# A four-layer graph network on one core: layer 3's passes over the edges get another order of work on each engine, a loop body of ten turns, and five shared PSUM banks in between

## The chip, the core and the metric

One core of a Trainium2 chip runs the whole program, 108212 recorded instructions. The metric is the device time of one execution in microseconds (us). TensorE is called PE here, VectorE DVE, ScalarE ACT, GpSimd POOL, and SyncE, which issues transfers, SP. An engine name with a q (DVEq) is that engine's sequencer, which handles register instructions, loads into registers and branches.

## What is computed

Four layers over a graph of N = 3125 nodes with 256 features and E = 50000 edges sorted by target. The change touches the graph part of layer 3, two rounds of this:

```python
k = (x @ Wk).reshape(n, H, D)   # H = 32 heads, D = 8
q = (x @ Wq).reshape(n, H, D)
v = (x @ Wv).reshape(n, H, D)
k_e, q_e, v_e = k[src], q[dst], v[src]
kw = where(is0, einsum('ehd,hdf->ehf', k_e, Watt[:, 0]), einsum(..., Watt[:, 1]))
m  = where(is0, einsum('ehd,hdf->ehf', v_e, Wmsg[:, 0]), einsum(..., Wmsg[:, 1]))
a  = (kw * q_e).sum(-1) * pri[:, etype].T / sqrt(D)
ea = exp(a - segment_max(a, dst)[dst])
att = ea / segment_sum(ea, dst)[dst]
h = segment_sum(m * att[:, :, None], dst).reshape(n, H * D) @ Wa
x = h * alpha + x * (1 - alpha)
```

## The kernel before

`hgt` runs each of the two rounds as an edge pass (`edge_pass` with kind "hgt"), a short join, and `renew`, which for the first round also makes the next round's table of keys and values and its queries. Gathered rows already hold the keys and messages of both edge types multiplied out, so a pass only gathers, scores, weighs and sums.

**The pass.** The 50000 edges lie in 416 tiles of 128, four tiles to a chunk, 104 chunks; one chunk is one turn. The work of turn k goes through the engines so: POOL gathers the chunk's rows from HBM into a ring `g` of NB = 4 chunks. SP fetches `locrow`, 256 KB (`hot`, line 764), and the masks. ACT turns `hot` into one-hot columns (lines 846 and 848). PE picks the queries with them (`queries`, line 805, eight matmuls, into `found`). DVE multiplies keys and queries (line 923) and sums by head (line 925). PE turns the scores into rows (line 813). DVE takes running maxima forwards and backwards (`scan` line 932, `scan_back` line 936). PE turns them back (line 820). DVE subtracts (`less`, lines 966 and 967), ACT takes exponents (line 861), DVE weighs the messages (`weigh`, line 974). PE sums them by node (`total`, line 831, eight matmuls in two halves), ACT copies the sums out of PSUM into `stage` (`take`, line 872), SP stores two of them (`keep`, line 769), and DVE adds them to the block of nodes in `acc` that the tile belongs to (`add`, line 988, four a turn). The block's number is loaded into a register from memory (`blocks_of`, line 667, one TENSOR_LOAD for all four), and each addition waits on a semaphore for the addition before it.

**The order.** Each engine has its order written out by hand, in `piped`: a list of stages, each with a lag in turns. Here is a turn of DVE before, as written:

```python
piped(v, NCH, [now(score), add(0), now(scan), add(1), now(scan_back), add(2), now(less), add(3), now(weigh(0))], NB)
```

`piped` writes the first turns out, then a hardware loop (`Fori`) whose body holds `unroll` turns, then the last ones. `unroll` was NB, so 4 turns here; layer 2's pass has a body of 8 turns, layer 0's one of 4. Translated, a body of DVE's has 133 instructions here, 494 in layer 2's pass and 239 or 247 in layer 0's two. `v.drain()` makes DVE wait until its own earlier operations have written their results.

**The renewal between the passes.** `renew` runs over 25 tiles of 125 nodes, in steps. PE transposes the sums (line 1961), multiplies by Wa (1969), transposes the new x (1977) and makes the 1280 new columns in three cuts of 512, 512 and 256 (1990, six matmuls a tile). DVE and ACT copy the cuts out of PSUM, and DVE counts s_take when its copies are done; PE waits for it and for ACT's s_half before the next tile's products, since there is one set of three banks. DVE also adds the old x (line 2105), between PE's 1969 and 1977.

Of the kernel before, what the change touches and what calls it, by code (L numbers as in the profile page):

```python
# [14 lines left out]
P = 125  # L15
# [31 lines left out]
def piped(eng, count, stages, unroll=4):  # L47
# [11 lines left out]
    with eng.Fori(first // unroll, last // unroll) as k:  # L59
        for u in range(unroll):  # L60
            step(unroll * k + u, u)
# [611 lines left out]
def edge_pass(core, name, kind, H, CT, acc, refs, crow, table, idx, look=None, early=None):  # L673
# [4 lines left out]
    NB = 8 if kind == "ee" else 4  # L678
# [7 lines left out]
    with Phase(core, name) as ph:  # L686
# [92 lines left out]
        def _(pe):  # L779
# [18 lines left out]
            def queries(k, b):  # L798
                blks = list(asked)
                pe.wait_ge(s_hot, k + 1)  # L800
                if later(k, 1):
                    pe.wait_ge(s_prod, k)
                for h in range(2):
                    for j in range(HT):
                        mm = pe.matmul(found[:, h, j * D:j * D + D], hot[0:P, b % 2, 128 * (h * HT + j):128 * (h * HT + j) + 128],  # L805
                                       look[:, bass.ds(blks[h * HT + j], 1), :].rearrange("p o c -> p (o c)"), start=True, stop=True)
                mm.then_inc(s_found, 1)
# [14 lines left out]
            def total(h):  # L822
                def body(k, b):
# [4 lines left out]
                    for t in range(h * HT, h * HT + HT):  # L828
                        if later(k, 1) or t >= 4:
                            pe.wait_ge(s_staged if kind == "hgt" else s_added, CT * k + t - 3)  # L830
                        pe.matmul(out[:, t % 4, 0:WO], here[:, b % 2, t, :], g[:, b, t, F:F + WO], start=True, stop=True).then_inc(s_out, 1)  # L831
# [3 lines left out]
            if kind == "ee":  # L835
                piped(pe, NCH, [(0, turn), (0, turn_back), (1, total(0)), (1, total(1))], NB)
            elif kind == "gat":
                piped(pe, NCH, [(1, turn), (2, total(0)), (1, turn_back), (0, find), (2, total(1))], NB)
            else:
                piped(pe, NCH, [(2, total(0)), (0, whose), (1, turn), (2, total(1)), (1, turn_back), (0, queries)], NB)  # L840

        @block.scalar
        def _(act):
# [32 lines left out]
            if kind == "gat":  # L876
                piped(act, NCH, [(3, take(0)), (2, exponent), (3, take(1)), (0, one_hot)], NB)
            elif kind == "hgt":
                piped(act, NCH, [(3, take(0)), (3, take(1)), (2, exponent), (0, one_hot), (1, rows_here)], NB)
            else:  # L880
                piped(act, NCH, [(0, exponent), (1, take(0)), (1, take(1))], NB)

        @block.vector
        def _(v):
# [16 lines left out]

            def score(k, b):
                v.wait_ge(s_g[b], every(k, b, NB, 16 * CT))
# [4 lines left out]
                if kind == "gat":  # L908
# [3 lines left out]
                    v.tensor_tensor(sums[:, :, :], sums[:, :, :], g[:, b, :, D:D + H], ALU.add)  # L912
# [2496 lines left out]
```

## Time and profile before

| | |
|---|---|
| median of 3 runs | 7328.54 us (7322.5 to 7334.62) |
| the profiled execution | 7332.78 us |
| its span on the core | 7330.6 us |
| granted TensorE clock, mean of the span | 0.867 of full |
| busy share: PE, DVE, ACT, POOL | 69%, 64%, 40%, 48% |

The first pass of layer 3 lies about between 4890 and 5626 us of the span, the renewal between 5703 and 5907, the second pass between 5907 and 6641. In a row of a timeline the columns are start, duration, engine, line, operation, out<-in, and in brackets the idle time before it with what ended it; durations of neighbours overlap a little, so that the distance between two starts is what an operation takes of the engine.

### The profile page before, as it was taken

The page shows a single profiled execution, that of the slowest core. Times are in us where ns is not written, and L with a number is a line of the kernel's source. Part 1 is how long each engine was busy: PE and PEld are TensorE (multiplying, and loading weights), DVE is VectorE, ACT ScalarE, POOL GpSimd, SP SyncE. Part 2 cuts the span into 40 slices and gives each one's busy share as a digit, 9 for nine tenths or more (in the row PEclk, how much of TensorE's full clock was granted, in tenths as well). Part 3 has the DMA queues.
Part 4 walks back from the last instruction along what each step waited for, and adds up shares of the span by engine and source line. Part 5 has one row for each costly group of instructions (what it writes and reads, how often), then busy time and mean ns, then how long its engine had stood idle before and what let it go on. Part 6 is the DMA issues. An engine that isn't in the chain of part 4 may idle for free. (4 is left out here: it accounts for less than half of the span.)

```text
span 7330.6 us, 108212 instructions
## 1 busy us (share of the span) xinstructions
PE 5055.0 (69%) x21503; PEld 3608.8 (49%) x21504; DVE 4711.4 (64%) x11833; ACT 2945.6 (40%) x7221; POOL 3519.8 (48%) x3532
## 2 busy tenths in 40 slices
PE   4763777767765967769666667777776767776764
PEld 4763444444444834558544457644444444444453
DVE  6876577667775168550566662379997379995453
ACT  2552355455544220022223332237775157773331
POOL 1776377447730267731167703336663056660014
PEclk9999977777777988979877778999999999997887
DMA  3442344334423943339334417756664167761036
GB/s 89 165 140 69 97 128 128 69 104 127 127 58 112 310 110 101 103 75 334 115 96 107 106 39 257 243 166 212 211 210 122 50 181 212 211 210 45 18 120 197
DMA packets 523817, 1021.67 MB, mean 139 GB/s; under 512 B 143645, under 2 KB 284498, under 8 KB 514846
## 3 DMA queue, kind: packets, MB, share of 16 engines
q0 software_dynamic: 191360, 489.21, 24.6%
q1 hardware_dynamic: 301663, 497.07, 21.0%
q10 hardware_dynamic: 30528, 32.52, 1.3%
q8 instruction: 86, 1.41, 0.1%
q14 instruction: 180, 1.47, 0.1%
HBM read 927.97 MB, written 90.27 MB: 139 GB/s over the span
## 5 line engine op out<-in xcount | busy, mean ns | idle before, releaser
L733 POOL DMA_INDIRECT l_hgt_ep_g<-l_tkm,l_hgt_ep_ix x832 | 922.4, 1109 | 441.3 <-PE l_hgt_ep_out L831 237.6
L744 POOL DMA_INDIRECT l_gat_ep_g<-l_gat_th,keep_e_src x832 | 863.4, 1038 | 439.8 <-issue 232.2
L831 PE MATMUL l_gat_ep_out<-l_gat_ep_g,l_gat_ep_here 128*126 128x264 f32 x1664 | 712.0, 570 | 137.4 <-DVE l_gat_acc L988 131.9
L831 PEld LDWEIGHTS l_gat_ep_out<-l_gat_ep_g,l_gat_ep_here 128*126 128x126 f32 x1664 | 387.8, 264 | 369.0 <-DVE l_gat_acc L988 301.7
L2495 DVE TENSOR_TENSOR f_moe_experts_yb<-f_moe_experts_py,f_moe_experts_b2s 128x256 f32<-128x256 f32 x208 | 88.4, 425 | 719.7 <-PE f_moe_experts_py L2478 700.7
L831 PE MATMUL l_hgt_ep_out<-l_hgt_ep_g,l_hgt_ep_here 128*126 128x288 f32 x1664 | 500.4, 424 | 53.8 <-DVE l_hgt_ep_g L974 52.3
L2446 POOL DMA_INDIRECT f_moe_experts_xg<-f_moe_tx,f_moe_tok x208 | 197.3, 949 | 708.2 <-PE f_moe_experts_px L2459 625.2
L872 ACT COPY l_gat_ep_stage<-l_gat_ep_out 30x264 f32<-30x264 f32 x832 | 306.3, 371 | 524.5 <-PE l_gat_ep_out L831 516.7
L2510 ACT ACTIVATE f_moe_experts_ht<-f_moe_experts_phid,f_moe_experts_b1b 128x128 f32<-128x128 f32 x848 | 241.3, 372 | 673.1 <-PE f_moe_experts_phid L2469 671.5
L525 POOL DMA_INDIRECT recs<-place_stage,place_pos x392 | 424.8, 1084 | 138.5 <-issue 117.1
L2831 POOL DMA_INDIRECT l_edges_g<-l_table,keep_e_src x416 | 412.3, 991 | 146.8 <-issue 119.8
L2469 PE MATMUL f_moe_experts_phid<-f_moe_experts_xt,f_moe_experts_w1b 128*128 128x128 f32 x3392 | 429.9, 281 | 74.5 <-DMA f_moe_experts_b1b<-in_L_ffn_b 66.3
L744 POOL DMA_INDIRECT l_ep_g<-l_table,keep_e_src x416 | 408.3, 982 | 126.6 <-issue 117.8
L2469 PEld LDWEIGHTS f_moe_experts_phid<-f_moe_experts_xt,f_moe_experts_w1b 128*128 128x128 f32 x3392 | 403.6, 195 | 95.8 <-issue 63.7
L805 PE MATMUL l_hgt_ep_found<-l_q,l_hgt_ep_hot 125*128 x1664 | 425.5, 400 | 26.0 <-ACT l_hgt_ep_hot L848 21.0
L2478 PE MATMUL f_moe_experts_py<-f_moe_experts_w2b,f_moe_experts_ht 128*128 128x256 f32 x1696 | 402.7, 381 | 0.0
L872 ACT COPY l_hgt_ep_stage<-l_hgt_ep_out 126x288 f32<-126x288 f32 x832 | 307.2, 394 | 218.3 <-PE l_hgt_ep_out L831 207.3
L988 DVE TENSOR_TENSOR l_gat_acc<-l_gat_acc,l_gat_ep_out 125x264 f32 x832 | 344.2, 414 | 68.8 <-issue 48.7
L988 DVE TENSOR_TENSOR l_hgt_acc<-l_hgt_acc,l_hgt_ep_stage 125x288 f32 x832 | 370.1, 445 | 20.9 <-ACT l_hgt_ep_stage L872 13.8
L831 PEld LDWEIGHTS l_hgt_ep_out<-l_hgt_ep_g,l_hgt_ep_here 128*126 128x126 f32 x1664 | 284.6, 190 | 181.1 <-issue 133.1
L2843 PE MATMUL l_edges_out<-l_edges_g,l_edges_here 128*125 128x256 f32 x832 | 254.1, 452 | 151.2 <-DVE l_acc L2930 49.0
L805 PEld LDWEIGHTS l_hgt_ep_found<-l_q,l_hgt_ep_hot 125*128 125x128 f32 x1664 | 306.5, 194 | 99.4 <-issue 62.9
(652 smaller groups left out, 11794.6 us busy)
## 6 DMA issues: line engine op xcount, KB each, us to landing
l_hgt_ep_hot<-locrow SPq DMA_DIRECT2D x208, 256.0 KB, 4.8
f_moe_experts_w1b<-in_L_ffn_w SPq DMA_DIRECT2D x32, 1024.0 KB
f_moe_experts_w2b<-in_L_ffn_w SPq DMA_DIRECT2D x32, 1024.0 KB
f_moe_experts_w1b<-in_L_ffn_w SPq DMA_DIRECT2D x64, 512.0 KB, 5.0
f_moe_experts_w2b<-in_L_ffn_w SPq DMA_DIRECT2D x64, 512.0 KB, 5.2
f_moe_experts_w1b<-in_L_ffn_W SPq DMA_DIRECT2D x56, 512.0 KB
f_moe_experts_w2b<-in_L_ffn_W SPq DMA_DIRECT2D x56, 512.0 KB
l_gat_ep_hot<-locrow SPq DMA_DIRECT2D x104, 256.0 KB
```

The costliest lines, as they stand in the source:

```text
L525: gp.indirect_dma_start(recs, bass.IndirectOffsetOnAxis(ap=pos[:, b, j:j + 1].bitcast(U32), axis=0), stage[:, b, j, :], None).then_inc(sca ...
L733: gp.indirect_dma_start(g[:, b % NB, j, 0:W], None, table, bass.IndirectOffsetOnAxis(ap=ix[:, b, j:j + 1].bitcast(U32), axis=0)).then_inc( ...
L744: gp.indirect_dma_start(g[:, k % NB, j, 0:W], None, table, bass.IndirectOffsetOnAxis(ap=idx[:, k * CT + j:k * CT + j + 1].bitcast(U32), ax ...
L805: mm = pe.matmul(found[:, h, j * D:j * D + D], hot[0:P, b % 2, 128 * (h * HT + j):128 * (h * HT + j) + 128], look[:, bass.ds(blks[h * HT + ...
L831: pe.matmul(out[:, t % 4, 0:WO], here[:, b % 2, t, :], g[:, b, t, F:F + WO], start=True, stop=True).then_inc(s_out, 1)
L872: act.copy(stage[lo:P + 1, b % 2, t, :], out[lo:P + 1, t % 4, 0:WO]).then_inc(s_staged, 1)
L988: v.tensor_tensor(slot, slot, stage[0:P, b % 2, t, :] if kind == "hgt" else out[0:P, t % 4, 0:WO], ALU.add).then_inc(s_added, 1)
L2469: mm = pe.matmul(phid[:, b % 2, 128 * f:128 * f + 128], w1b[:, b, k, 128 * f:128 * f + 128], xt[:, b % 2, k, :], start=(k == 0), stop=(k = ...
L2478: mm = pe.matmul(py[:, b % 2, 0:D], ht[:, b % 2, f, :], w2b[:, b, f, :], start=(f == 0), stop=(f == FC - 1))
L2510: act.activation(ht[:, b % 2, f, :], phid[:, b % 2, 128 * f:128 * f + 128], func, bias=b1b[:, b, f:f + 1])
L2831: gp.indirect_dma_start(g[:, i % RB, j, :], None, table, bass.IndirectOffsetOnAxis(ap=core.e_src[:, i * EG + j:i * EG + j + 1].bitcast(U32 ...
L2843: pe.matmul(out[:, j, 0:D], here[:, i % 4, j, :], g[:, i % RB, j, :], start=True, stop=True).then_inc(s_out, 1)
```

## The change

A turn of DVE: the chunk's messages are weighed one turn later, right behind the next chunk's scores; the additions stand in pairs behind `scan_back` and behind `less`, tiles 2 and 3 one turn later than before, and each pair loads its own two block numbers. PE makes the queries in two halves, one before the rows are turned and one at the turn's end, and its sums in halves one turn later. ACT copies one half of the sums first in its turn and the other one before the exponents. The ring `g` has five chunks, and the loop's body ten turns, with 350 instructions on DVE. POOL's and SP's orders and lags stay. In the renewal the five banks of PSUM that hold cuts are given out in turn, (3t + n) mod 5, each cut with a semaphore of its own, and the two other products have one bank each where they had one or two.

```diff
-    NB = 8 if kind == "ee" else 4
+    NB = {"ee": 8, "gat": 4, "hgt": 5}[kind]
+    UN = 10 if kind == "hgt" else NB
...
-            def queries(k, b):
-                blks = list(asked)
-                pe.wait_ge(s_hot, k + 1)
-                if later(k, 1):
-                    pe.wait_ge(s_prod, k)
-                for h in range(2):
+            def queries(h):
+                def body(k, b):
+                    if h == 0:
+                        pe.wait_ge(s_hot, k + 1)
+                        if later(k, 1):
+                            pe.wait_ge(s_prod, k)
...
-                mm.then_inc(s_found, 1)
+                    if h == 1:
+                        mm.then_inc(s_found, 1)
+                return body
...
-                piped(pe, NCH, [(2, total(0)), (0, whose), (1, turn), (2, total(1)), (1, turn_back), (0, queries)], NB)
+                piped(pe, NCH, [(3, total(1)), (0, whose), (0, queries(0)), (1, turn), (2, total(0)), (1, turn_back), (0, queries(1))], UN)
...
-                piped(act, NCH, [(3, take(0)), (3, take(1)), (2, exponent), (0, one_hot), (1, rows_here)], NB)
+                piped(act, NCH, [(4, take(1)), (2, rows_here), (3, take(0)), (2, exponent), (0, one_hot)], UN)
...
-                    v.drain()
-                    v.tensor_reduce(r, g[:, b, :, 0:D].rearrange("p t (h d) -> p t h d", h=H), AX.X, ALU.add).then_inc(s_raw, 1)
+
+            def by_head(k, b):
+                v.drain()
+                v.tensor_reduce(raw[:, b % 2, :, :], g[:, b % NB, :, 0:D].rearrange("p t (h d) -> p t h d", h=H), AX.X, ALU.add).then_inc(s_raw, 1)
...
-                    n = HT if kind != "hgt" else CT
-                    if t % n == 0:
-                        blks[t:t + n] = blocks_of(core, mybir.EngineType.DVE, k * CT + t, n)
+                    if t % HT == 0:
+                        blks[t:t + HT] = blocks_of(core, mybir.EngineType.DVE, k * CT + t, HT)
...
-                return (2 if t >= HT and kind != "hgt" else 1), body
+                return (2 if t >= HT else 1), body
...
-                piped(v, NCH, [now(score), add(0), now(scan), add(1), now(scan_back), add(2), now(less), add(3), now(weigh(0))], NB)
+                piped(v, NCH, [now(score), now(by_head), (1, weigh(0)), now(scan), now(scan_back), add(2), add(3), now(less), add(0), add(1)], UN, turns)
...
-                        if t >= B1:
+                        if t >= B1 and not shared:
                             pe.wait_ge(s_take, t - B1 + 1)
...
+                            if shared and len(cuts) * t + n >= 5:
+                                before, cut = divmod(len(cuts) * t + n - 5, len(cuts))
+                                pe.wait_ge((s_first, s_half, s_take)[cut], before + 1)
```

On DVE, in the loop of the passes, a turn stood so before (ISA here is a register instruction, TENSOR_LOAD the load of block numbers):

```order
L923 TENSOR_TENSOR l_hgt_ep_g<-l_hgt_ep_g,l_hgt_ep_found 128x4x256
L925 TENSOR_REDUCE l_hgt_ep_raw<-l_hgt_ep_g 128x128
L667 ISA
L667 TENSOR_LOAD keep_e_blk
L984 REGISTER_ALU
L988 ISA
L988 TENSOR_TENSOR l_hgt_acc<-l_hgt_acc,l_hgt_ep_stage 125x288
L932 SCALAR_TENSOR_TENSOR l_hgt_ep_fwd<-l_hgt_ep_masks,l_hgt_ep_rows 128x128
L984 REGISTER_ALU
L988 ISA
L988 TENSOR_TENSOR l_hgt_acc<-l_hgt_acc,l_hgt_ep_stage 125x288
L936 SCALAR_TENSOR_TENSOR l_hgt_ep_top<-l_hgt_ep_masks,l_hgt_ep_fwd 128x128
```

and after `scan_back` came:

```order
L984 REGISTER_ALU
L988 ISA
L988 TENSOR_TENSOR l_hgt_acc<-l_hgt_acc,l_hgt_ep_stage 125x288
L966 TENSOR_TENSOR l_hgt_ep_x<-l_hgt_ep_raw,l_hgt_ep_back 128x128
L967 ISA
L967 COPY l_hgt_refs<-l_hgt_ep_top 128x2
L984 REGISTER_ALU
L988 ISA
L988 TENSOR_TENSOR l_hgt_acc<-l_hgt_acc,l_hgt_ep_stage 125x288
L974 TENSOR_TENSOR l_hgt_ep_g<-l_hgt_ep_g 128x4x256
```

After the change a turn begins so (lines are 10 to 13 higher):

```order
L933 TENSOR_TENSOR l_hgt_ep_g<-l_hgt_ep_g,l_hgt_ep_found 128x4x256
L937 TENSOR_REDUCE l_hgt_ep_raw<-l_hgt_ep_g 128x128
L986 TENSOR_TENSOR l_hgt_ep_g<-l_hgt_ep_g 128x4x256
L941 ISA
L944 SCALAR_TENSOR_TENSOR l_hgt_ep_fwd<-l_hgt_ep_masks,l_hgt_ep_rows 128x128
L948 SCALAR_TENSOR_TENSOR l_hgt_ep_top<-l_hgt_ep_masks,l_hgt_ep_fwd 128x128
L669 ISA
L669 TENSOR_LOAD keep_e_blk
L995 REGISTER_ALU
L999 ISA
L999 TENSOR_TENSOR l_hgt_acc<-l_hgt_acc,l_hgt_ep_stage 125x288
L995 REGISTER_ALU
```

and ends so:

```order
L999 TENSOR_TENSOR l_hgt_acc<-l_hgt_acc,l_hgt_ep_stage 125x288
L978 TENSOR_TENSOR l_hgt_ep_x<-l_hgt_ep_raw,l_hgt_ep_back 128x128
L979 ISA
L979 COPY l_hgt_refs<-l_hgt_ep_top 128x2
L669 ISA
L669 TENSOR_LOAD keep_e_blk
L995 REGISTER_ALU
L999 ISA
L999 TENSOR_TENSOR l_hgt_acc<-l_hgt_acc,l_hgt_ep_stage 125x288
L995 REGISTER_ALU
L999 ISA
L999 TENSOR_TENSOR l_hgt_acc<-l_hgt_acc,l_hgt_ep_stage 125x288
```

The weighing has moved up behind the reduction, and the additions, each of which stood between two other operations, stand in two pairs. The one load behind the reduction has become two, one behind `scan_back` and one behind the copy.

On PE a turn of the loop stood so before:

```order
L831 MATMUL l_hgt_ep_out<-l_hgt_ep_g,l_hgt_ep_here 126x288
L667 ISA
L667 TENSOR_LOAD keep_e_blk
L813 MATMUL l_hgt_ep_rows<-keep_ident,l_hgt_ep_raw 128x128
L830 REGISTER_ALU
L831 MATMUL l_hgt_ep_out<-l_hgt_ep_g,l_hgt_ep_here 126x288 x2
L820 MATMUL l_hgt_ep_back<-keep_ident,l_hgt_ep_top 128x128
L800 REGISTER_ALU
L805 ISA
L805 MATMUL l_hgt_ep_found<-l_q,l_hgt_ep_hot 128x256
L805 ISA
L805 MATMUL l_hgt_ep_found<-l_q,l_hgt_ep_hot 128x256
```

and stands so now:

```order
L804 REGISTER_ALU
L808 ISA
L808 MATMUL l_hgt_ep_found<-l_q,l_hgt_ep_hot 128x256
L808 ISA
L808 MATMUL l_hgt_ep_found<-l_q,l_hgt_ep_hot 128x256
L817 REGISTER_ALU
L818 MATMUL l_hgt_ep_rows<-keep_ident,l_hgt_ep_raw 128x128
L835 ISA
L836 MATMUL l_hgt_ep_out<-l_hgt_ep_g,l_hgt_ep_here 126x288
L835 REGISTER_ALU
L836 MATMUL l_hgt_ep_out<-l_hgt_ep_g,l_hgt_ep_here 126x288
L825 MATMUL l_hgt_ep_back<-keep_ident,l_hgt_ep_top 128x128
```

Two of the four products of the queries (L808) have moved ahead of the turned rows (L818); the other two come right behind the last row shown, behind the turned maxima (L825), where all four stood before (L805, the first two shown).

## Rows read from the trace of the kernel before

**Rows 1.** Windows of the trace: the first pass, and the renewal between passes (busy us, clock).

```profile
4890.00:5626.00 736.00, 512.04 (x1873) 318.75 (x1874) 663.17 (x1145) 513.94 (x1249) 486.69 (x518) 0.98 0.68 205
5703.00:5907.00 204.00, 153.36 (x500) 87.96 (x500) 54.33 (x103) 30.76 (x75) 0.00 (x0) 0.94 0.20 62
```

**Rows 2.** Groups by line on DVE, 4950 to 5550: busy, mean ns, idle before.

```profile
L988 DVE TENSOR_TENSOR l_hgt_acc<-l_hgt_acc,l_hgt_ep_stage 125x288 f32 x351 | 155.8, 444 | 3.6 <-ACT l_hgt_ep_stage L872 0.8
L925 DVE TENSOR_REDUCE l_hgt_ep_raw<-l_hgt_ep_g 128x128 f32<-128x1024 f32 x88 | 107.4, 1220 | 8.0
...
L932 DVE TENSOR_TENSOR_SCAN l_hgt_ep_fwd<-l_hgt_ep_masks,l_hgt_ep_rows 128x128 f32<-128x128 f32 x88 | 37.0, 421 | 7.6 <-PE l_hgt_ep_rows L813 3.9
```

**Rows 3.** Timeline of DVE, one turn: start, duration, operation.

```profile
5208.49 1.22 DVE L923 TENSOR_TENSOR l_hgt_ep_g<-l_hgt_ep_g,l_hgt_ep_found 128x1024 f32<-128x1024 f32 x1
5209.81 1.22 DVE L925 TENSOR_REDUCE l_hgt_ep_raw<-l_hgt_ep_g 128x128 f32<-128x1024 f32 x1
5210.94 0.45 DVE L988 TENSOR_TENSOR l_hgt_acc<-l_hgt_acc,l_hgt_ep_stage 125x288 f32 x1
5211.45 0.42 DVE L932 TENSOR_TENSOR_SCAN l_hgt_ep_fwd<-l_hgt_ep_masks,l_hgt_ep_rows 128x128 f32<-128x128 f32 x1
...
5212.31 0.42 DVE L936 TENSOR_TENSOR_SCAN l_hgt_ep_top<-l_hgt_ep_masks,l_hgt_ep_fwd 128x128 f32<-128x128 f32 x1
5212.65 0.43 DVE L988 TENSOR_TENSOR l_hgt_acc<-l_hgt_acc,l_hgt_ep_stage 125x288 f32 x1
5213.22 0.29 DVE L966 TENSOR_TENSOR l_hgt_ep_x<-l_hgt_ep_raw,l_hgt_ep_back 128x128 f32<-128x128 f32 x1
...
5213.61 0.46 DVE L988 TENSOR_TENSOR l_hgt_acc<-l_hgt_acc,l_hgt_ep_stage 125x288 f32 x1
5213.99 1.22 DVE L974 TENSOR_TENSOR l_hgt_ep_g<-l_hgt_ep_g 128x1024 f32<-128x1024 f32 x1
5215.23 1.22 DVE L923 TENSOR_TENSOR l_hgt_ep_g<-l_hgt_ep_g,l_hgt_ep_found 128x1024 f32<-128x1024 f32 x1
```

**Rows 4.** Timeline of DVE in layer 0's pass: a load behind a short operation.

```profile
1613.84 0.19 DVE L914 SCALAR_TENSOR_TENSOR l_gat_ep_raw<-l_gat_ep_sums 128x32 f32<-128x32 f32 x1
1614.43 0.43 DVE L988 TENSOR_TENSOR l_gat_acc<-l_gat_acc,l_gat_ep_out 125x264 f32 x1 [0.40 <-issue]
```

**Rows 5.** Instructions of line 667, 4950 to 5550: ns least, median, most.

```profile
L667 DVEq TENSOR_LOAD <-keep_e_blk x88: 339/344/357, 4950.0 to 5546.7; - x88
```

**Rows 6.** Timeline of DVE in layer 0's pass: additions in a row.

```profile
1398.87 0.43 DVE L988 TENSOR_TENSOR l_gat_acc<-l_gat_acc,l_gat_ep_out 125x264 f32 x1 [0.21 <-DVE l_gat_acc L988]
1399.51 0.43 DVE L988 TENSOR_TENSOR l_gat_acc<-l_gat_acc,l_gat_ep_out 125x264 f32 x1 [0.21 <-DVE l_gat_acc L988]
```

**Rows 7.** Instructions of line 59 (loop), layer 2's pass: ns, start us.

```profile
L59 DVEq COMPARE_BRANCH  x1: 73/73/73, 3947.8 to 3947.8; - x1
...
L59 DVEq FUSED_REGOPS  x1: 80/80/80, 3950.8 to 3950.8; - x1
```

**Rows 8.** The same line in layer 3's first pass.

```profile
L59 DVEq COMPARE_BRANCH  x1: 56/56/56, 5008.8 to 5008.8; - x1
L59 DVEq FUSED_REGOPS  x1: 74/74/74, 5009.2 to 5009.2; - x1
```

**Rows 9.** Line 764's transfer of locrow, 5000 to 5580: us to landing.

```profile
DMA to landing us min/median/max: 3.5/4.8/6.4
```

**Rows 10.** Groups by line on ACT, 4950 to 5550.

```profile
L872 ACT COPY l_hgt_ep_stage<-l_hgt_ep_out 126x288 f32<-126x288 f32 x352 | 129.9, 394 | 89.1 <-PE l_hgt_ep_out L831 84.8
...
L848 ACT ACTIVATE l_hgt_ep_hot<-l_hgt_ep_hot,keep_ones 128x512 f32<-128x512 f32 x87 | 62.8, 722 | 6.0
```

**Rows 11.** Timeline of PE in the renewal: two starts of one tile's products.

```profile
5780.39 4.53 PE L1990 MATMUL l_hgt_out_out<-l_w,l_hgt_out_xt 128*125 128x512 f32 x12 [1.62 <-DVEq L2154]
...
5787.84 0.67 PE L1990 MATMUL l_hgt_out_out<-l_w,l_hgt_out_xt 128*125 128x512 f32 x1 [1.62 <-DVEq L2154]
```

**Rows 12.** The same, late in the renewal.

```profile
5888.54 4.53 PE L1990 MATMUL l_hgt_out_out<-l_w,l_hgt_out_xt 128*125 128x512 f32 x12 [1.04 <-ACT l_hgt_out_rows L2026]
```

More of the change, by code:

```diff
@@ L44, in later, with piped @@
     return not isinstance(i, int) or i >= n
-def piped(eng, count, stages, unroll=4):
+def piped(eng, count, stages, unroll=4, turns=None):
     first = -(-(max(lag for lag, _ in stages) + unroll) // unroll) * unroll
@@ L59, in piped @@
     with eng.Fori(first // unroll, last // unroll) as k:
+        if turns is not None:
+            turns[:] = [k]
         for u in range(unroll):
@@ L830, in body @@
                             pe.wait_ge(s_staged if kind == "hgt" else s_added, CT * k + t - 3)
-                        pe.matmul(out[:, t % 4, 0:WO], here[:, b % 2, t, :], g[:, b, t, F:F + WO], start=True, stop=True).then_inc(s_out, 1)
+                        pe.matmul(out[:, t % 4, 0:WO], here[:, b % 2, t, :], g[:, b % NB, t, F:F + WO], start=True, stop=True).then_inc(s_out, 1)
                 return body
@@ L900, in _ @@
             v.drain()
+            turns = [None]
             def score(k, b):
-                v.wait_ge(s_g[b], every(k, b, NB, 16 * CT))
+                if isinstance(k, int):
+                    v.wait_ge(s_g[b % NB], 16 * CT * (k // NB + 1))
+                else:
+                    v.wait_ge(s_g[b % NB], turns[0] * (16 * CT * UN // NB) + 16 * CT * (b // NB + 1))
                 if later(k):
@@ L1854, in renew @@
     mixed = part["acc"] if part else xn
-    B0, B1 = (1, 1) if part and wide else (2, 2)
+    shared = part is not None and wide
+    B0, B1 = 1 if shared else 2, 2
     last_on_vector = onward.get("last") if wide else None
@@ L1892, in renew, with made_in @@
             xt1 = kept_xt if kept_xt is not None else ph.sb("xt1", [128, 2, 2, P])
-            pt1 = ph.psum("pt1", [128, 2, 512])
-            out1 = ph.psum("out1", [P, B1, len(cuts), 512])
+            pt1 = ph.psum("pt1", [128, B0, 512])
+            out1 = ph.psum("out1", [P, 1, 5, 512] if shared else [P, B1, len(cuts), 512])
+            s_cut = [ph.sem(f"cut{n}") for n in range(2)] if shared else []
+            s_first = ph.sem("first") if shared else None
+            def made_in(t, n, c):
+                return out1[:, 0, (len(cuts) * t + n) % 5, 0:c] if shared else out1[:, t % B1, n, 0:c]
             w, dst = onward["w"], onward["dst"]
@@ L2104, in _ @@
                         v.wait_ge(s_mm0, t + 1)
-                        o = v.scalar_tensor_tensor(out=x[:, t, :], in0=part["old"][:, t, :], scalar=part["rest"], in1=out0[:, t % 2, 0:D], op0=ALU.mult, op1=ALU.add)
+                        o = v.scalar_tensor_tensor(out=x[:, t, :], in0=part["old"][:, t, :], scalar=part["rest"], in1=out0[:, t % B0, 0:D], op0=ALU.mult, op1=ALU.add)
                         if back is not None:
```

66 lines of the change are left out of this document (36 added, 30 removed).

## The prediction

> **What bounds the kernel now.** The page gives no engine more than 69% of the span, so I looked only at the stretches that the change touches. The view by windows shows a pass of 736.00 us in which DVE is busy 663.17 and PE 512.04, at clock 0.98, and a renewal of 204.00 in which PE is busy 153.36 and DVE only 54.33 [rows 1]. The groups by line then show that DVE in the pass waits almost for nothing: the 351 additions have 3.6 us of idle time before them in 600 us, the reduction comes 88 times with 8.0, and the scan waits 3.9 of its 7.6 us for PE [rows 2]. So a turn is 600/88 = 6.82 us, and it is the sum of DVE's own row of instructions. The timeline of one turn reads it off [rows 3]: from the product at 5208.49 to the next one at 5215.23, 6.74 us. What DVE's order costs is what the passes cost, 2 x 104 turns.
>
> **A turn, laid out anew.** I take distances between starts from [rows 3].
> - Product to reduction, with the drain between them, stays 1.32.
> - The weighing behind the reduction: reduction to the next start was 1.13, take 1.14. It starts at 2.45.
> - The scan behind the weighing: the weighing is as large as the reduction, another 1.14, start 3.59. Its rows have been turned meanwhile: PE had 0.51 us for that before (addition 5210.94 to scan 5211.45) and has 1.14 now. That ends the wait for PE.
> - scan_back behind the scan and a drain: the scan takes 0.42, and the drain a little more, start 4.09.
> - First addition of the pair (tile 2). Before it stands a load of two block numbers that nothing covers. A load takes 339 to 357 ns on DVE's sequencer [rows 5]. Before, it lay under the reduction of 1.22 us. Now it comes behind scan_back, whose 0.42 us are too short for load, register arithmetic and the wait on a semaphore. Layer 0's pass has the same place: an operation of 0.19 us at 1613.84, a load, and the addition only at 1614.43, with 0.40 idle [rows 4], so that the chain from one start to the other is 0.59. Here the register arithmetic of `acc`'s address and the wait for `stage` may come on top: at most as much again as a load, 0.34, so between 0.59 and 0.93. I take the middle, an estimate of 0.755, against 0.34 before (5212.31 to 5212.65). Start 4.845; **+0.41** for the load.
> - Second addition (tile 3). It waits for the semaphore of the one before it. In layer 0's pass, where additions stand in a row, each has 0.21 idle before it and starts 0.64 behind the last [rows 6], where the distance between an addition and another operation is 0.34 to 0.38 here [rows 3]. The old order had another operation of 0.29 or more between any two additions. Start 5.485; **+0.29**.
> - less 0.35 later, 5.835 (before, from 5212.65 to 5213.22, it came 0.57 behind the addition: 0.22 was a wait for PE's turned-back maxima, which is gone: **-0.22**). Less and copy together take 0.39 (to the addition at 5213.61).
> - First addition of the second pair (tile 0): another load, issued when the copy has been handed over, about 5.65; by the chain of 0.755 with two operations in a row handed over it starts at about 6.5, against 6.25 (5.835 + 0.39) without a load: **+0.25**.
> - Second addition (tile 1): 0.64 behind, 7.15; **+0.29**.
> - Next product 0.36 behind: 7.50. Gone are what the scan waited (0.13 to 0.2) and the 0.1 by which the weighing and the next product stood further apart than 1.14 (5213.99 to 5215.23).
>
> Old turn 6.82, plus 0.41 + 0.29 + 0.25 + 0.29 = 1.24, minus 0.22, 0.16, 0.10 and some 0.1 that the drained scan_back gains without an addition ahead of it, is about 7.5. I take 7.50; the bounds: both loads hidden 6.95 to 7.0, and both chains as long as with nothing below them 7.7.
>
> **Another ring stands close.** ACT's take of the second half is now first in its turn, behind the one-hot. SP keeps its order, so that the store of tile 3 of chunk k-3 stands ahead of the next fetch of locrow. That makes one ring a turn: take 0.7 (two of 0.394), fetch 4.8 to landing (3.5 to 6.4), one-hot two of 0.722, with issue 1.5 [rows 9, 10], and about 0.65 of stores' issue: 7.65 with 4.8, 6.35 with 3.5, 9.25 with 6.4. Before, the same ring took two turns of DVE. So 7.50 may become a little more; I take 7.55 as a mean, +0.72 for each of the 80 loop turns of a pass, 2 x 80 x 0.72 = **+115**. The other 24 turns of a pass are written out; they load and wait alike, but I leave out what the fetch ring adds and a part of the second load: 2 x 24 x 0.55 = **+26**.
>
> **The loop's end.** The body of ten turns has 350 instructions on DVE, and the jump back is taken 7 times a pass. In layer 2's pass, with 494, the branch at 3947.8 is followed by the next register instruction only at 3950.8, 2.9 us of nothing [rows 7]; in layer 3's with 133, from 5008.8 to 5009.2 [rows 8]. 350 lies between the two, and no row tells on which side. [...] Its 2.9 us and some 0.4 until the turn is back in step, 3.3, come 14 times: **+46**; at the short one's price it is +7. The old loop ended 24 times a pass with some 0.2 us, which the new one does 7 times: **-6**.
> [...]
>
> **The renewal.** PE begins one tile's products at 5780.39 and the next at 5787.84, 7.45 apart, with 1.62 idle right before, ended by DVE's count of its copies [rows 11]; late in the stretch the wait is 1.04 [rows 12]. With five banks the first cut of the next tile needs only a bank that was emptied a tile before. Both waits go; what PE has of its own is 7.45 - 1.62 = 5.83. Of 25 tiles the first five run while the line fills: 15 x 1.62 + 4 x 1.04 = 28, and where one wait is gone the copies at the end run sooner and PE's gap behind DVE's addition of the old x closes a little: I take **-37**, between -30 and -42. What hides there is nothing: PE is the bound of that stretch.
>
> Ring of five chunks: POOL is busy 486.69 of 736.00 [rows 1] and no DVE row waits for a gather, so it gives nothing. Queries in halves: no DVE row of a turn waits for them.
>
> **Sum.** 115 + 26 + 46 - 6 - 37 = +144 on the profiled execution's 7332.78, 7477; the median of the runs shown lies 4 lower, so 7473. I say **7470**.
>
> **Rivals.**
> - *Faster.* The waits that go (for rows, for turned-back maxima, before the product) are worth 0.5, and the loads lie under their neighbours because the sequencer runs ahead. If also half of the self-waits is hidden, a turn takes 6.5: 208 x -0.32 = -67, and -37 gives 7225; with a turn as before only the renewal is left, 7292. It decides where the turn stays below 6.82 + 37/208 = 7.00 (without misses). Against it stand both costs, shown in the same operation [rows 4, 6]. 0.13.
> - *No change.* Loads hidden, self-waits only: a turn of 6.85, +6, +46 for the jumps, -37: 7343; 0.05.
> - *The fetch ring or PE sets the turn.* With landings near 6 us a turn is 8 to 8.3: 160 x 1.3 + 26 + 46 - 43 = +237, 7566. For it: 256 KB a turn beside the gathers. Against it: the median of 4.8, and fewer transfers per us in a slower turn. 0.12.
> - *The jump is cheap*, all else as forecast: -39, 7431. [...] Within the forecast's range: 0.25.
> - The forecast itself, with misses: 0.45.
>
> **How the numbers follow.** About 0.2% (15 us) is what a measurement can tell from no change. Slower: 0.45 + 0.25 + 0.12 = 0.82; same 0.05; faster 0.13. The bounds of the turn, 7.3 to 7.7, and of the jumps give 7390 to 7510 for the likeliest; to reach 8 in 10 the range takes in some of the ring's case: 7365 to 7560.
>
> **What the new profile would show.** The first addition behind scan_back 0.7 to 0.8 us after scan_back's start, with about 0.3 idle; the second with 0.21 idle ended by DVE's own addition; no scan row that waits for PE; a gap of 3 us on DVE every ten turns; DVE busy less than before in a longer pass; steps of 5.8 us in the renewal. I would be wrong if additions in pairs stand 0.35 apart, if the load's 0.34 us don't show, or if the one-hot waits for its transfer in most turns.

## The result, and the profile after

The changed kernel takes 7608.79 us (median of 4, 7607.7 to 7613.77) where the kernel before takes 7330.1 on the same chip: 1.0381 of it, with a 95% interval of 1.0365 to 1.0398. The forecast was 7470, in a range of 7365 to 7560; the kernel became slower, as forecast, but by 279 us in place of 140, and lies outside the range. One later execution of the changed kernel (in e5) took 8743.67 us at a granted clock of 0.575; the comparisons rest on the others.

The profiled execution has a span of 7606.5 us against 7330.6, 275.9 more. Measured from DVE's first key product (line 923 before, 933 after) to its last one, a pass has grown from 713.9 to 875.9 us and from 708.6 to 867.9, together by 321. The stretch between the passes has shrunk from 306.7 to 264.4. The rest of the program, before and after, makes -3. So everything lies where the change is, and the two parts of it have opposite signs.

The windows of the first pass, the counterpart of [rows 1] (busy us with counts, granted clock, share of the DMA engines, GB/s):

```profile
4901.00:5777.00 876.00, 588.04 (x1846) 386.31 (x1846) 656.28 (x1127) 508.95 (x1228) 478.39 (x510) 0.84 0.58 170
```

DVE is busy for about as long as before (656 against 663), but in 876 us in place of 736: it waits. PE does the same products in 588 where it had 512, at a granted clock of 0.84 in place of 0.98. Both were to be explained. What DVE waits for stands in its waits over the same stretch (us in total, times, longest):

```profile
DVE l_hgt_acc L999 <- issue: 102.6, 201, 1.1
DVE l_hgt_acc L999 <- DVE l_hgt_acc L999: 31.2, 145, 0.2
DVE l_hgt_ep_g L933 <- issue: 25.5, 7, 5.2
DVE l_hgt_ep_raw L937 <- issue: 14.4, 7, 2.9
DVE l_hgt_acc L999 <- ACT l_hgt_ep_stage L877: 13.1, 59, 0.7
DVE l_hgt_ep_x L978 <- PE l_hgt_ep_back L825: 12.1, 38, 1.1
```

Before, all these together had 3.6 us in front of the additions in 600 [rows 2]. Now the additions have 147 in 876, in three rows. The largest row says "issue", a wait for nothing that the profile shows, about twice a turn, half a microsecond each. The second is an addition that waits for the addition before it. The rows with 7 times are the seven jumps of the loop, and in this pass each jump has two of them. In the second pass (6030 to 6910) only the first of the two is there:

```profile
DVE l_hgt_ep_g L933 <- issue: 26.4, 7, 4.6
```

One turn on DVE, the counterpart of [rows 3] (start, duration, operation, idle before it):

```profile
5210.22 1.21 DVE L933 TENSOR_TENSOR l_hgt_ep_g<-l_hgt_ep_g,l_hgt_ep_found 128x1024 f32<-128x1024 f32 x1
5211.52 1.22 DVE L937 TENSOR_REDUCE l_hgt_ep_raw<-l_hgt_ep_g 128x128 f32<-128x1024 f32 x1
5212.66 1.22 DVE L986 TENSOR_TENSOR l_hgt_ep_g<-l_hgt_ep_g 128x1024 f32<-128x1024 f32 x1
5213.79 0.41 DVE L944 TENSOR_TENSOR_SCAN l_hgt_ep_fwd<-l_hgt_ep_masks,l_hgt_ep_rows 128x128 f32<-128x128 f32 x1
5214.28 0.42 DVE L948 TENSOR_TENSOR_SCAN l_hgt_ep_top<-l_hgt_ep_masks,l_hgt_ep_fwd 128x128 f32<-128x128 f32 x1
5215.21 0.46 DVE L999 TENSOR_TENSOR l_hgt_acc<-l_hgt_acc,l_hgt_ep_stage 125x288 f32 x1 [0.51 <-issue]
5215.89 0.46 DVE L999 TENSOR_TENSOR l_hgt_acc<-l_hgt_acc,l_hgt_ep_stage 125x288 f32 x1 [0.22 <-ACT l_hgt_ep_stage L877]
5216.27 0.28 DVE L978 TENSOR_TENSOR l_hgt_ep_x<-l_hgt_ep_raw,l_hgt_ep_back 128x128 f32<-128x128 f32 x1
5216.46 0.17 DVE L979 COPY l_hgt_refs<-l_hgt_ep_top 128x2 f32 x1
5217.07 0.46 DVE L999 TENSOR_TENSOR l_hgt_acc<-l_hgt_acc,l_hgt_ep_stage 125x288 f32 x1 [0.45 <-issue]
5217.75 0.46 DVE L999 TENSOR_TENSOR l_hgt_acc<-l_hgt_acc,l_hgt_ep_stage 125x288 f32 x1 [0.22 <-DVE l_hgt_acc L999]
5218.13 1.21 DVE L933 TENSOR_TENSOR l_hgt_ep_g<-l_hgt_ep_g,l_hgt_ep_found 128x1024 f32<-128x1024 f32 x1
```

It is 7.91 us. Up to scan_back at 4.06 behind the product it is the forecast's turn to a few hundredths. Then the first addition comes 0.93 behind scan_back (forecast 0.755), and the one behind the copy 0.61 behind it. The cause stands in the instructions of the line that loads the block numbers (ns least, median, most; DVEq is DVE's sequencer):

```profile
L669 DVEq TENSOR_LOAD <-keep_e_blk x127: 520/536/555, 5005.2 to 5549.3; - x127
...
L669 PEldq TENSOR_LOAD <-keep_e_blk x63: 328/332/352, 5006.0 to 5542.4; - x63
```

DVE's load of two numbers takes 0.536 us, where its load of four took 0.344 [rows 5]; PE's load, still of four, is where it was, at 0.332.

In other turns PE stands in the way. Here are PE's rows of the turn before, and of this one:

```profile
5205.56 2.28 PE L836 MATMUL l_hgt_ep_out<-l_hgt_ep_g,l_hgt_ep_here 128*126 128x288 f32 x4 [0.67 <-DVE l_hgt_ep_g L986]
5207.64 0.42 PE L825 MATMUL l_hgt_ep_back<-keep_ident,l_hgt_ep_top 128*128 128x128 f32 x1
...
5214.11 1.23 PE L836 MATMUL l_hgt_ep_out<-l_hgt_ep_g,l_hgt_ep_here 128*126 128x288 f32 x4 [0.98 <-DVE l_hgt_ep_g L986]
5215.18 0.27 PE L825 MATMUL l_hgt_ep_back<-keep_ident,l_hgt_ep_top 128*128 128x128 f32 x1
```

The same products (L836) take 2.28 and 1.23 us: the granted clock was 0.50 from 5205.5 to 5207.9 and 1.00 from 5214.0 to 5215.5. In the slow one the maxima are turned back so late that `less` waits 0.31 and the load behind it starts later; that turn is 8.55 us. I sorted the turns by the duration of the row L825 (0.42 and 0.27 in these two): 82 at the half clock have a mean of 8.38, 103 at the full one 7.905 (turns over 9.2 left out). Ahead of the half-clock rows PE had waited 2.3 us for DVE's product (median), ahead of the full-clock ones 1.2.

The end of a loop's body, on DVE's timeline:

```profile
5400.73 0.46 DVE L999 TENSOR_TENSOR l_hgt_acc<-l_hgt_acc,l_hgt_ep_stage 125x288 f32 x1 [0.22 <-DVE l_hgt_acc L999]
5404.90 1.22 DVE L933 TENSOR_TENSOR l_hgt_ep_g<-l_hgt_ep_g,l_hgt_ep_found 128x1024 f32<-128x1024 f32 x1 [3.71 <-issue]
5408.56 1.22 DVE L937 TENSOR_REDUCE l_hgt_ep_raw<-l_hgt_ep_g 128x128 f32<-128x1024 f32 x1 [2.43 <-issue]
```

Behind the branch at 5400.8 the next register instruction comes at 5404.5, and a few instructions on DVE stalls again: five instructions have run, and the sixth, the drain ahead of the reduction, starts only at 5408.4. The page's list of queues shows the same from another side: the queue of kind instruction, q14, has 267 packets where it had 180. Around this jump, from 5398 to 5412, it has three:

```profile
q14 instruction: 3, 0.02, 0.5%
```

In the trace they have 8192 bytes each and start at 5402.7, 5406.6 and 5409.1: one ahead of the first instruction behind the branch, one ahead of the drain. At all 14 jumps of the two passes the second packet behind the branch starts 2.4 to 4.5 us behind the first one, which has taken 0.3 to 0.7.

In the renewal, PE's rows of the five-bank rotation:

```profile
5931.90 4.46 PE L2010 MATMUL l_hgt_out_out<-l_w,l_hgt_out_xt 128*125 128x512 f32 x12
...
5937.50 4.46 PE L2010 MATMUL l_hgt_out_out<-l_w,l_hgt_out_xt 128*125 128x512 f32 x12
```

They begin 5.60 apart with no wait before them, where they began 7.45 apart [rows 11].

### The profile page after: what moved, and what is told of

Same layout as the page of the kernel before. It is cut to its first block and busy times, and to the rows that moved or that the text cites. A ratio compares the mean times of both kernels' runs of the same rounds, so it can differ in the third digit from the quotient of the medians.

```text
span 7606.5 us, 107407 instructions
## 1 busy us (share of the span) xinstructions
PE 5238.5 (69%) x21503; PEld 3766.9 (50%) x21504; DVE 4733.1 (62%) x11833; ACT 2955.5 (39%) x7221; POOL 3510.8 (46%) x3532
## 5 line engine op out<-in xcount | busy, mean ns | idle before, releaser
L736 POOL DMA_INDIRECT l_hgt_ep_g<-l_tkm,l_hgt_ep_ix x832 | 896.3, 1077 | 768.1 <-PE l_hgt_ep_out L836 538.0
L808 PE MATMUL l_hgt_ep_found<-l_q,l_hgt_ep_hot 125*128 x1664 | 551.4, 463 | 412.0 <-DVE l_hgt_ep_g L933 391.1
L836 PE MATMUL l_gat_ep_out<-l_gat_ep_g,l_gat_ep_here 128*126 128x264 f32 x1664 | 717.8, 576 | 136.2 <-DVE l_gat_acc L999 132.0
L836 PE MATMUL l_hgt_ep_out<-l_hgt_ep_g,l_hgt_ep_here 128*126 128x288 f32 x1664 | 619.9, 505 | 175.4 <-DVE l_hgt_ep_g L986 126.1
L808 PEld LDWEIGHTS l_hgt_ep_found<-l_q,l_hgt_ep_hot 125*128 125x128 f32 x1664 | 347.7, 232 | 582.8 <-issue 534.3
L836 PEld LDWEIGHTS l_gat_ep_out<-l_gat_ep_g,l_gat_ep_here 128*126 128x126 f32 x1664 | 389.2, 266 | 370.3 <-DVE l_gat_acc L999 306.2
L836 PEld LDWEIGHTS l_hgt_ep_out<-l_hgt_ep_g,l_hgt_ep_here 128*126 128x126 f32 x1664 | 368.3, 234 | 316.3 <-issue 197.2
```

What stands on the lines that cost most here:

```text
L736: gp.indirect_dma_start(g[:, b % NB, j, 0:W], None, table, bass.IndirectOffsetOnAxis(ap=ix[:, b, j:j + 1].bitcast(U32), axis=0)).then_inc( ...
L836: pe.matmul(out[:, t % 4, 0:WO], here[:, b % 2, t, :], g[:, b % NB, t, F:F + WO], start=True, stop=True).then_inc(s_out, 1)
```

## The experiments

Two chips ran the parts of the program that no kernel here touches slower than the others: that of e1 to e4 (the first pass began at 5437 us in place of 4899, the kernel before took 7919 us) and that of e12 (7931 us). In e4, whose passes have the old order, 24 of the 206 turns took over 8 us, where the kernel before had 4, and the passes took 1485 us in place of 1422.5. So of these runs the traces' turns are compared more than the totals. "Pass 1 + 2" below is measured from the first key product to the last, as above: 1422.5 before, 1743.9 after.

**e1, loads of four.** Each pair loads all four numbers of its chunk and uses two.

```diff
-                        blks[t:t + HT] = blocks_of(core, mybir.EngineType.DVE, k * CT + t, HT)
+                        blks[:] = blocks_of(core, mybir.EngineType.DVE, k * CT, CT)
```

> The changed kernel, but each pair of additions loads all four block numbers of its chunk and uses two. Theory A (a load of two numbers is itself the slow thing, 0.52 to 0.54 us where loads of four take 0.34): the loads fall to 0.34, the plain turn from 7.90 to about 7.52, the total by 208 x 0.38 = 79 us to about 7530. Rival B (what is exposed behind scan_back is the waiting for ACT's stage or register work, not the load's length): loads may change, the first addition of a pair stands where it stood, total 7609 within 15 us.

Measured: 8097.36, 1.0229 of before on its chip. The loads:

```profile
L669 DVEq TENSOR_LOAD <-keep_e_blk x120: 340/344/359, 5699.9 to 6199.1; - x120
```

They fall from 0.536 to 0.344 us though they fetch twice as much, and the plain turn from 7.90 to 7.42. Passes 1686, 58 less, with 24 turns over 9.2 us in them, up to 14.3. Theory A holds: it is the load of two that is slow. The address is no rival: one of the two loads of a turn reads from the same place in both kernels, and all 127 took 520 ns or more. Two loads shorter by 0.19 make 0.38 of the 0.48; the edit also saves a register instruction a turn (341 in a body in place of 350), and how much of the other 0.1 that is, no run separates. Why two numbers take longer than four, no run here shows.

**e2, ring and body of four.**

```diff
-    NB = {"ee": 8, "gat": 4, "hgt": 5}[kind]
-    UN = 10 if kind == "hgt" else NB
+    NB = {"ee": 8, "gat": 4, "hgt": 4}[kind]
+    UN = NB
```

> The changed kernel with a ring of four chunks and a loop body of four turns. Theory A (the jump back of the long body costs 5.5 us each, 7 a pass, in two stalls of fetching): the two idle stretches of DVE at a jump vanish, 14 x 5.5 = -77, and the short one's 0.2 comes 48 times, +10: about 7540. Rival B (the fifth chunk feeds the gathers in time, since weighing a turn later holds rows longer): DVE's products wait for gathers, the gain is lost or turned, 7600 or more.

Measured: 8110.01, 1.0239 of before. The stalls at the jumps are gone (no jump over 0.3 us), the turns stay 7.90 and 8.55. Passes 1706, 38 less (on that chip). The turn is as long with four chunks as with five, so the fifth chunk buys nothing.

**e3, sums twice.** The products of tiles 2 and 3 are made twice in each turn, the first ones for nothing.

```diff
+                        if kind == "hgt" and h == 1:
+                            pe.matmul(out[:, t % 4, 0:WO], here[:, b % 2, t, :], g[:, b % NB, t, F:F + WO], start=True, stop=True)
                         pe.matmul(out[:, t % 4, 0:WO], here[:, b % 2, t, :], g[:, b % NB, t, F:F + WO], start=True, stop=True).then_inc(s_out, 1)
```

> The changed kernel with PE's sums of tiles 2 and 3 of each chunk made twice (the same products into the same bank, the second one counted), so that PE has four products more in the stretch in which it waits for DVE's product. Theory A (every other turn is 8.55 instead of 7.90 because PE's granted clock falls to half in PE's idle stretches and its turned-back maxima come late): the granted clock in the pass rises from 0.83 to 0.95 or more, the turns of 8.55 mostly go, about 100 of them x 0.65: 7609 - 60 = 7550. Rival B (PE's amount of work is what is late): more turns of 8.55 and longer ones, 7640 or more.

Measured: 8177.59, 1.0309. The clock in the pass rises only to 0.87, and 58 turns of 170 are at the half clock, mean 8.36, against 112 at 7.92; but 36 turns are over 9.2 us (mean 11.4) in place of 21, and the passes take 1783. Neither theory's numbers came out. It was taken up again in e11 without the jumps.

**e4, the renewal alone.** The kernel before with the five banks: the changed kernel with

```diff
-    UN = 10 if kind == "hgt" else NB
+    UN = NB          # and a ring of 4
...
-  [now(score), now(by_head), (1, weigh(0)), now(scan), now(scan_back), add(2), add(3), now(less), add(0), add(1)]
+  [now(score), now(by_head), add(0), now(scan), add(1), now(scan_back), add(2), now(less), add(3), now(weigh(0))]
```

and the old orders of PE and ACT, one load of four and the old lag of the additions.

> The kernel before with only the renewal's five shared banks. The distance between the last product of pass 1 and the first of pass 2 was 306.7 before and is 264.5 after: if that is the banks alone, 7330 - 42 = 7288. Rival: part of the 42 is the pass's new end (fewer additions left over), then 7290 to 7310.

Measured: 7896.69, 0.9975 of before (0.9954 to 0.9996). Between the passes the trace has 263.9, against 264.4 in the changed kernel: the banks do all of it, 43 us. The total shows only 23, on a chip whose executions of one kernel spread by 48.

**e5, the changed kernel again**, as the measure for e6 to e8.

> The changed kernel itself once more, as the measure for the other three of this chip. Both theories: 0.5 to 4% slower than the kernel before; its turns in the trace as in the first profile, 7.90 at full clock and 8.4 at half, two stalls at each jump.

Measured: 7615.28, 1.0385 of the kernel before (7332.46). Turns as before: 83 at the half clock with 8.38, 101 at the full one with 7.92. As in the first profile, the seven jumps of the first pass have two stalls each and those of the second pass one each, not two everywhere as expected.

**e6, the old order with a long body.** The kernel before with the five banks and UN = 12, 396 instructions on DVE; against e4:

```diff
-    UN = NB
+    UN = 12 if kind == "hgt" else NB
```

> The kernel before with the five shared banks, and its old order of a turn, but a loop body of 12 turns (399 instructions on DVE), jump back 6 times a pass. Theory A (a long body must be fetched anew at each jump, 3.2 us at the branch and 2.3 us some instructions later): 12 x 5.5 = +66 against the renewal alone, less some 8 for the short jumps it no longer has: 0.8% over it, so about 7346 where that is 7288. Rival (the stalls belong to the new order, in which DVE has no work queued at a jump): no idle stretch over 1 us at the branch, same time as the renewal alone.

Measured: 7380.36, 1.0067 of before; without the long body it should have been 43 us under it. Passes 1509.8, 87 more than before, over ten jumps 8.7 us each, where 5.5 were expected. Most of its turns are 6.74 to 7.03 as before; at the jumps they are 10.7 to 11.3 in the first pass and 14.6 to 15.1 in the second, and 8.2 to 8.6 behind. In the second pass, and not in the first, a second stall of 3.2 to 3.4 us stands a few instructions behind the jump. The branch:

```profile
L59 DVEq COMPARE_BRANCH  x1: 68/68/68, 5149.0 to 5149.0; - x1
...
L59 DVEq FUSED_REGOPS  x1: 62/62/62, 5154.2 to 5154.2; - x1
```

So the stalls belong to the long body, in whatever order; the rival falls.

**e7, e1 and e2 together.**

> The changed kernel with both mended: loads of four numbers, ring and body of four. If load length, jumps and clock are all there is apart from the pairs' own waits: turn 7.43 at full clock, 8.3 at half clock in a quarter of the turns, mean 7.65, no stall at a jump; passes 2 x 103 x (8.47 - 7.65) = 169 us shorter than the changed kernel, still 100 us longer than before (pairs waiting on themselves, loads in the open). Rival (ring of four holds it back): mean turn 7.9 or more.

Measured: 7477.28, 1.0199 of before, some 135 under the changed kernel. Passes 1613.5, mean turn 7.83, 0.18 more than expected: 73 turns are still at the half clock, a third and not a quarter. The waits of its first pass:

```profile
DVE l_hgt_acc L1001 <- issue: 59.2, 199, 0.5
DVE l_hgt_acc L1001 <- DVE l_hgt_acc L1001: 40.2, 188, 0.2
```

Even loads of four stand in the open for 0.3 us each, and each pair waits for itself once, 0.21.

**e8, single additions.** Loads and additions as far as possible where something covers them, PE's queries ahead of its sums, all additions two turns behind with one load of four numbers, the store of tiles 2 and 3 one turn later, ring and body of four.

```diff
-  [now(score), now(by_head), (1, weigh(0)), now(scan), now(scan_back), add(2), add(3), now(less), add(0), add(1)]
+  [now(score), add(0), now(by_head), add(1), (1, weigh(0)), now(scan), now(scan_back), add(2), now(less), add(3)]
...
-  [(3, total(1)), (0, whose), (0, queries(0)), (1, turn), (2, total(0)), (1, turn_back), (0, queries(1))]
+  [(3, total(1)), (0, whose), (0, queries(0)), (1, turn), (0, queries(1)), (2, total(0)), (1, turn_back)]
```

> A version meant to be fast: weighing one turn later as in the change, but the four additions each between two other operations, one load of four numbers behind the product that covers it, all two turns behind; PE makes both halves of the queries ahead of the sums; the store of tiles 2 and 3 one turn later on SP; ring and body of four; five shared banks. If the loads in the open and the additions' waits on each other are what the change lost, and its removed waits are a real gain: turn 6.3 to 6.45, passes 206 x 0.45 = 90 us shorter than before, and 43 of the renewal: 1.8% faster than before. Rival (PE, the gathers or the fetch of locrow then set the turn): 6.8 or more, no faster than the renewal alone.

Measured: 7300.44, 0.9958 of before (0.9942 to 0.9975). Neither open load nor waiting pair is left, but the turn is 6.79: `less` waits for PE, which sums tiles 0 and 1 ahead of turning back.

```profile
5206.52 0.29 DVE L978 TENSOR_TENSOR l_hgt_ep_x<-l_hgt_ep_raw,l_hgt_ep_back 128x128 f32<-128x128 f32 x1 [0.44 <-PE l_hgt_ep_back L825]
```

So PE decides, as in the rival. The passes take 1430.4, 8 more than before: the whole gain, 32 us, is the renewal's.

**e9, pairs with an early load.** Body of four, the pairs kept, but one load behind the product. It also gives both pairs the lag of two turns and puts tiles 0 and 1 first, so that it differs from e7 by more than the load.

```diff
-  [now(score), now(by_head), (1, weigh(0)), now(scan), now(scan_back), add(2), add(3), now(less), add(0), add(1)]
+  [now(score), (2, numbers), now(by_head), (1, weigh(0)), now(scan), now(scan_back), add(0), add(1), now(less), add(2), add(3)]
```

> Ring and body of four, order of a turn as in the change, but one load of four numbers behind the product that covers it, and the two pairs of additions both two turns behind. It differs from load4_body4 (7477, turn 7.43 at full clock) by the open loads alone. Theory A (open loads of 0.34 are still 0.5 us of a turn, the pairs' waits on themselves 0.43): turn 6.9 at full clock, 7477 - 206 x 0.5 = 7375 or less if the half clock goes too. Rival (the first addition of a pair has other waits, ACT's stage or the registers): turn over 7.2, 7430 or more.

Measured: 7387.28, 1.0056 of before. Its full-clock turn has a median of 6.82, the clock in the window 4950 to 5550 is 0.95, and only 28 turns are at the half clock. The addition behind scan_back comes at 0.35 again, the second one of the pair still waits:

```profile
5208.40 0.42 DVE L948 TENSOR_TENSOR_SCAN l_hgt_ep_top<-l_hgt_ep_masks,l_hgt_ep_fwd 128x128 f32<-128x128 f32 x1
5208.75 0.43 DVE L999 TENSOR_TENSOR l_hgt_acc<-l_hgt_acc,l_hgt_ep_stage 125x288 f32 x1
5209.39 0.46 DVE L999 TENSOR_TENSOR l_hgt_acc<-l_hgt_acc,l_hgt_ep_stage 125x288 f32 x1 [0.21 <-DVE l_hgt_acc L999]
```

Covering the loads was worth up to 0.61 us of a full-clock turn (7.43 to 6.82), and with them went most of the half clock. In total it lies 12 above the expected; its chip runs the kernel before 9 us slower than e7's, and in the first pass the scan waited 33 us for PE in 26 turns.

**e10, e8 with the maxima turned back first.**

```diff
-  [(3, total(1)), (0, whose), (0, queries(0)), (1, turn), (0, queries(1)), (2, total(0)), (1, turn_back)]
+  [(3, total(1)), (0, whose), (0, queries(0)), (1, turn), (0, queries(1)), (1, turn_back), (2, total(0))]
```

> The version of e8_singles with one thing changed: PE turns the maxima back ahead of its sums of tiles 0 and 1, since there DVE's subtraction waited 0.44 us a turn for PE, whose sums stood in front. If that wait is all that held it at 6.79: turn 6.4, 7300 - 206 x 0.4 = 7218. Rival (another ring is just behind, ACT's or the fetch of locrow): turn 6.6 or more, 7260 or more.

Measured: 7242.11, 0.9864 of before (0.9847 to 0.988): 99.5 us faster than the kernel before on its chip, the fastest of all. The turn is 6.48 (median), passes 1364.6. The window 4950 to 5550:

```profile
4950.00:5550.00 600.00, 413.47 (x1645) 279.03 (x1645) 562.53 (x1003) 438.23 (x1097) 436.25 (x457) 1.00 0.76 220
```

DVE is busy 563 of 600, clock 1.00. Of the 0.1 that the turn lies over the expected 6.4 nothing is waited for in DVE's rows but 0.09 at the reduction's drain.

**e11, e7 with the sums twice**, the edit of e3 in the kernel of e7.

> load4_body4 (73 of 205 turns at half clock, mean 8.28, the others 7.56) with PE's sums of tiles 2 and 3 made twice. Theory (PE's idle stretches bring the clock down, and the half clock costs 0.7 us a turn): fewer turns at half clock, below 40, full-clock turns unchanged at 7.4 to 7.6, total 7477 - 25 = 7450. Rival (it is the work, or the clock doesn't mind four products): as many turns at half clock, 7477 or more.

Measured: 7466.77, 1.0168 of a kernel before of 7341.64; e7 was 1.0199. In the window 4950 to 5550 the clock is 0.94 in place of 0.89, 55 turns are at the half clock in place of 73, and full-clock turns are as they were. The passes take 1600.0 in place of 1613.5. More work for PE made the kernel no slower, if anything 0.3% faster: less idle time of PE goes with less of the half clock. The size is smaller than expected (below 40 turns).

**e12, e10 with a body of eight turns**, 265 instructions on DVE.

```diff
-    UN = NB
+    UN = 8 if kind == "hgt" else NB
```

> The version of e10_back_first (7242) with a loop body of eight turns, 265 instructions on DVE, in place of four turns with 134. If 265 are still held at the jump: half of the loop's ends, each 0.42 us (6.90 instead of 6.48), go: 7242 - 24 x 0.42 = 7232. If a body of 265 is fetched anew: about 22 jumps in both passes, each 5.5 us or more instead of 0.4, less those 10: 7340 or more. So it tells on which side of the step 265 lies, where 247 was held, and 350 and 396 were not.

Measured: 8075.8, 1.0178 of before. All ten jumps of either pass stall, 20 of 20. The first one:

```profile
L59 DVEq COMPARE_BRANCH  x1: 73/73/73, 5618.3 to 5618.3; - x1
...
L59 DVEq FUSED_REGOPS  x1: 63/63/63, 5623.0 to 5623.0; - x1
```

Turns at a jump are 11.7 to 15.4 and 8.7 to 10.7 behind; the others have a median of 6.48. A second stall follows each jump: in the first pass ahead of the seventh recorded instruction of the body, the TENSOR_LOAD, in the second ahead of the sixth, the register instruction in front of it. The two bodies start 1025 recorded instructions of DVE apart, so the two places of the second stall are 1024 apart: it does not stand at one place of the loop. What sets its place no run shows. In the kernel before, the bodies of 239 and 247 instructions jump back in 0.2 to 0.3 us, each of 10 times; this one of 265 takes 4.4 to 6.4.

## Why the prediction was right in direction and too small in size

**The bound and the way to read it** held: DVE's row of instructions is the pass, and its order is most of what the change costs.

**The moved weighing.** Right: scan at 3.57 behind the product (forecast 3.59), the wait for turned rows gone, scan_back at 4.06 (4.09).

**"First addition of the pair" with its "estimate of 0.755", "+0.41", and the second load, "+0.25".** This is the step that failed most. I took the load's duration from a load of four numbers and never asked whether one of two costs the same, though a halved load was the change (all 624 of DVE's loads of block numbers in the kernel before are of four). It takes 0.19 us longer (e1), which put the chain at 0.93. That is the upper end that I had given, but by luck: I had given it for register work and the wait for `stage`. The second load put its addition 0.61 behind the copy in place of 0.2, +0.41. With the spacings of 0.67 in a pair the turn became 7.905, not the 7.54 of the sum (6.82 + 0.72): 160 loop turns x 0.365 = 58 us. The written-out turns hold the same loads: their 46 distances have a mean of 7.73, in all 42 us more than 46 x 6.82, where the sum had 26: 16 more.

**The additions' wait on each other, +0.29 each.** Right: 0.21 of waiting at each, spacing 0.67 (forecast 0.64); the same 0.21 in e7 and e9, absent in e8 and e10.

**"-0.22", for the wait for PE's turned-back maxima.** Right at full clock, wrong in the other 82 turns. That PE would lose its clock was not in the forecast's sum; it stood in the heading of a rival with no mechanism. The old pass had it at 0.98 [rows 1], and I carried that over although the new turn, by its own working, left PE idle for longer. 82 x (8.38 - 7.905) = 39 us in both passes. The loop's turns away from the jumps have a mean of 8.23, 0.33 over the full-clock turn: 160 x 0.33 = 52, of which the half clock is the greater part. That PE's idle time brings it is supported by e11, which took it only from 73 turns to 55, and by the clock of 1.00 in e10, which changes the whole order; what share of a turn must be idle is open.

**The fetch of locrow, "7.65".** Wrong, though small: landing has a median of 3.8 us in the slower pass, and ACT's one-hot waits for it twice in the first pass, 0.6 us in all. The 0.05 that I added to the turn for it was nothing.

**The loop's end, "3.3, come 14 times".** No row showed whether a body of 350 jumps back like that of 133 or like that of 494; giving it the long one's price, 2.9 us, was the author's estimate. The side came out right, the size did not. By the turns around the jumps the seven of the first pass cost 42 us, with two stalls each, and the seven of the second 29, with one each: 71 in place of 46.

What these runs show, from the branch to the next instruction on DVE: bodies of 239 and 247 jumped back in 0.2 to 0.3 us (before, 20 jumps), one of 265 in 4.4 to 6.4 (e12, 20), one of 350 in 2.7 to 5.1 (the changed kernel, 14) and one of 494 in 2.8 to 3.0 (before, 3, one of them in [rows 7]). At those of 341 it took 3.0 to 6.7 (e1, 14), and at those of 396 DVE had nothing to do for 3.6 to 4.4 (e6, 10). No packet of q14 starts within 10 us behind any of the 20 jumps of 239 and 247; behind each of the 14 of 350 at least two do. So in these runs the step from a short jump to a stall lies between 247 and 265. Whether length alone sets it is open.

The forecast has no second stall. In the changed kernel the body has the same code in both passes, and the second packet starts 2.4 to 4.5 us behind the first at all 14 jumps; yet the stall comes at the seven of the first pass alone. Why is not shown.

**The renewal, -37.** Right, 43 measured (e4), with steps of 5.60 in place of the 5.83 that I had left for PE.

**Ring of five and queries in halves: nothing.** For the ring right (e2); for the queries in halves no run separates it.

Together, in the passes: 58 for the full-clock turn, 52 for what the loop's turns lie above it, 16 for the written-out turns and 25 for the jumps make 151. To these come 6 that I took off for the old loop's ends and that are no term of their own here. Off go 18, because the old passes took 1422.5 and not 206 x 6.82 = 1405 (their dear last turns, up to 11.5, which I left out of the base). That leaves 139 or 140, and the passes grew by 321 where the sum had 181. The renewal brought 5 more than the 37, and the rest of the program took 3 less. So the profiled execution is 132 over the 7477 that the sum gave for it; the other 7 of the 139 are the steps from 7477 down to 7470.

Was weighing later bad? Not in company that suits it: e10 keeps it, covers the load, parts the additions and lets PE turn back first, and its passes are 58 us shorter than before. No run moves the weighing alone, so its own share is not shown. The change paired it with loads in the open, additions in pairs and a long body, which cost more than it brings.

## What to carry to other kernels

When a register load is moved, look at what runs above it: under an operation of 1.2 us it was free here (all 351 additions before had 3.6 us of idle time [rows 2]), behind one of 0.4 all or most of its length showed (0.59 us for a load of 0.54, 0.3 for one of 0.34), and its length must be measured for the number of values that it loads. Operations that each wait for the one before on the same engine, 0.21 us each here, belong apart, with something else between. Count the instructions of a loop's body per engine before unrolling it further (247 jumped back in 0.3 us, 265 in 4.4 or more), and when an engine's partner becomes slower, ask what its own clock will do (PE's fell from 0.98 to 0.84 here).

## What the runs showed of the hardware that was not expected

- A load of two numbers into DVE's registers took 0.536 us (127 of them, 520 to 555 ns), one of four from the same array 0.344.
- A body of 265 instructions on DVE stalled at every jump (20 of 20), bodies of 239 and 247 at none. In the changed kernel the stall between the branch and the next instruction took 2.7 to 5.1 us.
- A second stall, 1.0 to 2.9 us of idle time in the changed kernel, came at every jump of its first pass and at none of its second, though the loop is the same; in e12 it came ahead of the body's seventh instruction in the first pass and ahead of its sixth in the second, 1024 recorded instructions further on.
- The packets of the instruction queue around a jump had 8192 bytes, and the second started 2.4 to 4.5 us behind the first (14 jumps of the changed kernel).
- More products on PE made the passes no longer (1613.5 to 1600.0 us) and the clock higher (0.89 to 0.94, e7 to e11).
